# Attention weights times V in row tiles of 64, V with a bank of its own, and a new timetable for the attention stage

## What is computed

```python
x = x + xattn(layernorm(x), ctx, ctx, wq, wk, wv, wo)
x = x + ffn(layernorm(x), W_in, b_in, W_out, b_out)

# xattn: 16 heads of 16 channels
Q, K, V = queries @ wq, keys @ wk, values @ wv        # to (batch, head, channel, time)
corr = irfft(rfft(Q) * conj(rfft(K)))                 # over 128 positions
top_vals, top_idx = top_k(corr, 4)                    # for each head and channel
w = softmax(top_vals)
for i in range(4):                                    # a roll along the 16 channels
    out = out + w[..., i] * take_along(V, (t - top_idx[..., i]) % 16)
return out @ wo

# ffn: 256 -> 1024 -> 256, int8 weights and int16 activations by the largest magnitude of the whole tensor
hidden = gelu(quantize_a16(x) @ quantize_w8(W_in) + b_in)
out = quantize_a16(hidden) @ quantize_w8(W_out) + b_out
```

## Time and profile before

| | us |
|---|---|
| median of 3 runs | 1089.81 |
| lowest and highest | 1086.69, 1091.14 |
| the profiled execution, device time | 1087.63 |
| its span, first to last instruction | 1085.8 |
| share of the span: PE, DVE, ACT, POOL | 97%, 89%, 86%, 46% |
| stage A, to the last `project_out` | 0 to 596.3 |
| seam 1 | 596.3 to 604.95 |
| stage B | 604.95 to 829.0 |
| seam 2 | 829.0 to 835.0 |
| stage C | 835.0 to 1085.8 |

### The profile page before, as it was taken

How to read it: one execution, slowest core, us unless ns; L and a number is a source line. 1 busy time by engine, 2 the same in 40 slices (tenths; PEclk the granted TensorE clock), 3 DMA queues, 4 the chain that set the end, 5 groups by cost and what they waited for, 6 DMA issues and landing times.

```text
span 1085.8 us, 28919 instructions
## 1 busy us (share of the span) xinstructions
PE 1048.4 (97%) x9303; PEld 772.8 (71%) x9303; DVE 969.8 (89%) x2790; ACT 936.6 (86%) x1698; POOL 504.7 (46%) x674
## 2 busy tenths in 40 slices
PE   6999999999999999999998799999997999999998
PEld 4787878878888888888876344444444888888886
DVE  3799989898888888889899899999997999999998
ACT  4787989988888888888888688888888999999996
POOL 4787888888888888888887300000000000000000
PEclk9999999999999999999999899999998999999999
DMA  5533335443334333333431499999899899999995
GB/s 184 162 117 94 121 114 142 113 124 119 124 116 133 118 119 117 119 118 117 118 119 49 144 302 303 302 302 302 305 305 378 298 346 342 343 341 344 339 348 199
DMA packets 141425, 222.59 MB, mean 205 GB/s; under 512 B 72320, under 2 KB 92160, under 8 KB 137216
## 3 DMA queue, kind: packets, MB, share of 16 engines
q1 hardware_dynamic: 140224, 220.12, 60.7%
q10 hardware_dynamic: 1088, 1.05, 0.3%
HBM read 121.00 MB, written 83.89 MB: 189 GB/s over the span
## 4 chain that ended last, share of the span: by engine, by line
PE 59%; DVE 10%; issue 8%; ACT 2%; DVEq 1%; POOL 0%; ACTq 0%; POOLq 0%
PE bank L596 21%; DVE arena L1436 6%; PE bank L431 5%; PE bank L444 5%; PE bank L506 5%; PE bank L482 5%; PE bank L625 4%; PE bank L456 4%; PE bank L494 4%; PE bank L468 3%; PE bank L521 3%; DVE arena L1429 2%; DVE arena L1451 1%; ACT arena L891 1%; DVEq L1433 0%
## 5 line engine op out<-in xcount | busy, mean ns | idle before, releaser
L625 PE MATMUL bank<-wout,arena 128*128 128x256 f16 x2048 | 236.3, 274 | 4.2 <-DVE arena L1429 3.0
L625 PEld LDWEIGHTS bank<-wout,arena 128*128 128x128 f16 x2048 | 197.0, 98 | 45.0 <-DVE arena L1436 10.6
L596 PE MATMUL bank<-arena,win 128*128 128x512 f16 x1024 | 224.1, 383 | 2.6 <-DVE arena L1387 2.6
L596 PEld LDWEIGHTS bank<-arena,win 128*128 128x128 f16 x1024 | 100.6, 98 | 126.0 <-issue 6.2
L1436 DVE SCALAR_TENSOR_TENSOR arena<-arena,wout_rel 128x512 f16<-128x512 int16 x256 | 183.0, 746 | 3.9 <-ACT arena L891 1.3
L848 ACT ACTIVATE arena<-bank,b_in_sb,z_scale 128x512 f32<-128x512 f32 x192 | 147.4, 778 | 16.4 <-PE bank L596 11.2
L711 ACT ACTIVATE arena<-arena 32x128 f32<-32x128 f32 x256 | 78.4, 306 | 57.7 <-DVE arena L1166 55.4
L645 ACT ACTIVATE arena<-bank 128x512 f32<-128x512 f32 (+1 forms) x196 | 115.3, 590 | 6.3 <-PE bank L431 2.9
L884 ACT ACTIVATE arena<-arena,one 128x1536 int16<-128x1536 f32 x64 | 100.2, 1568 | 18.3 <-DVE arena L1436 15.3
L645 ACT ACTIVATE arena<-arena 128x512 f16<-128x512 f32 x192 | 112.9, 618 | 1.2 <-POOL arena L951 1.1
L1401 DVE TENSOR_REDUCE hmax<-arena 128x1 f32<-128x1024 f32 x96 | 111.2, 1211 | 2.9 <-ACT arena L848 2.9
(11 more groups left out here) (121 smaller groups left out, 2040.7 us busy)
## 6 DMA issues: line engine op xcount, KB each, us to landing
hidden_scratch<-arena SPq DMA_DIRECT2D x32, 1536.0 KB, 5.6
arena<-hidden_scratch SPq DMA_DIRECT2D x64, 768.0 KB, 7.1
arena<-in_ctx_turned SPq DMA_DIRECT2D x64, 256.0 KB, 2.7
arena<-in_x_turned SPq DMA_DIRECT2D x64, 256.0 KB, 2.8
arena<-in_x SPq DMA_DIRECT2D x64, 256.0 KB, 3.7
x_scratch<-arena SPq DMA_DIRECT2D x64, 256.0 KB, 3.5
arena<-x_scratch SPq DMA_DIRECT2D x32, 512.0 KB, 6.0
out<-arena SPq DMA_DIRECT2D x32, 512.0 KB, 4.3
```

Source lines behind the costliest of these rows:

```text
L596: last = nc.tensor.matmul(bank[f][:, :].rearrange("p (n t) -> p n t", n=4), win16[:, f, c, :], xt[q % 3][:, s, :, c, :], start=s == 0 and ...
L625: last = nc.tensor.matmul(bank[m * 2 + k // 2][:, k % 2 * D:(k % 2 + 1) * D], gbuf[:, s, f, k * P:(k + 1) * P], wout16[:, f, :], start=f = ...
```

## The change

`attend` becomes eight matmuls in place of four. The mixing matrix `mt` is zero outside blocks on its diagonal, so its upper and lower halves of 64 rows need only 64 columns each. Each half is a matmul with a contraction of 64, still with 128 columns of weights (V) but 64 moved columns. The upper half writes into the free columns 256 to 511 of bank 5, the lower into those of bank 6, and the two banks are now one PSUM tensor `both`, so that ScalarE can read the two halves in one instruction. V keeps bank 7 for itself.

```diff
-        bank = [ctx.enter_context(nc.psum_tensor(f"bank{n}", [P, 512], F32)) for n in range(8)]
+        both = ctx.enter_context(nc.psum_tensor("both", [P, 1024], F32))
+        bank = [ctx.enter_context(nc.psum_tensor(f"bank{n}", [P, 512], F32)) for n in (0, 1, 2, 3, 4, 7)]
+        bank[5:5] = [both[:, 0:512], both[:, 512:1024]]
+        mixed = lambda h: bank[5 + h][:, 2 * P:4 * P].rearrange("p (c b l) -> p c b l", c=2, b=2)
+        mixed_halves = both[:, :].rearrange("p (h s k l) -> p h s k l", h=2, s=2, k=4)[:, :, 1]
...
# project_v
-                wait(pe, S["ot_out"], upto(p - 3) if taken is None else taken)
...
# attend
-                wait(pe, S["vt_out"], upto(p + 4) if taken is None else taken)
+                wait(pe, S["top_done"], upto(p + 2) if taken is None else taken)
                 for c in range(DC):
                     for b in range(2):
-                        last = nc.tensor.matmul(four(7)[:, c, b, :], vt[:, p, c, b, :], mt[:, c, b, :], start=True, stop=True)
+                        for h in range(2):
+                            half_of = slice(h * NF, (h + 1) * NF)
+                            last = nc.tensor.matmul(mixed(h)[:, c, b, :], vt[half_of, p, c, b, :], mt[half_of, c, b, half_of], start=True, stop=True)
...
# inverse
+                wait(pe, S["ot_out"], upto(p - 1) if taken is None else taken)
...
# high_ot, and take_ot alike
-                copy(ot16[p % 2][:, 0].rearrange("p c b l -> p (c b l)"), bank[7][:, :], "ot_high")
+                copy(ot16[p % 2][:, 0].rearrange("p c b (h l) -> p h (c b) l", h=2), mixed_halves, "ot_high")
```

TensorE's step is put in another order with other lags:

```diff
-                if active(t, 0):
-                    project_k(t)
-                    project_v(t)
-                if active(t, 4):
-                    project_out(t - 4)
-                if active(t, 0):
-                    if t == 0:
-                        mean_of_wq()
-                    project_q(t)
-                if active(t, 3):
-                    attend(t - 3)
-                if active(t, 0):
-                    dft_k(t)
-                    dft_q(t)
-                if active(t, 1):
-                    inverse(t - 1)
+                if active(t, 5):
+                    attend(t - 5)
+                if active(t, 2):
+                    dft_q(t - 2)
+                    dft_k(t - 2)
+                if active(t, 3):
+                    inverse(t - 3)
+                if active(t, 1):
+                    project_k(t - 1)
+                    project_v(t - 1)
+                    project_q(t - 1)
+                if active(t, 5):
+                    project_out(t - 5)
```

The work on the feed-forward weights moves. On VectorE all of it falls into two steps, on ScalarE it is one operation a step over 24 steps:

```diff
-W_STEP = 6
+W_STEP = 4
...
# VectorE, weights(t)
+                if t == 2:
                     dve.wait_ge(S["w_in_loaded"], 16)
+                    for k in range(4):
+                        largest_w(w_in_raw, win_max, k)
+                    scales(win_max, win_up).then_inc(S["w_in_scaled"], 1)
+                if t == 3:
                     dve.wait_ge(S["w_out_in"], 16)
+                    for k in range(4):
+                        largest_w(w_out_raw, wout_max, k)
                     link(scales(wout_max, wout_up))
...
# ScalarE, weights(t)
+                k, r = (t - W_STEP) // 3, (t - W_STEP) % 3
+                if 0 <= k < 4:
+                    scaled_w_in(2 * k + r) if r < 2 else stage_w_in(k)
+                if 4 <= k < 8:
+                    scaled_w_out(2 * (k - 4) + r) if r < 2 else stage_w_out(k - 4)
```

TensorE gets matmuls whose result nobody reads: ten at the start, ahead of `mean_of_wq` (which now runs first, and `wq` is loaded second in place of third), 13 and 8 in seam 1, 4 and 10 in seam 2:

```diff
+            def keep_warm(n, k, table_of=None):
+                lhs, rhs = (minus_mean, minus_mean) if table_of is None else (inv16[:, 0, 0, :], inv16.rearrange("p s k t -> p (s k t)"))
+                for _ in range(k):
+                    nc.tensor.matmul(bank[n][:, 0:rhs.shape[-1]], lhs, rhs, start=True, stop=True)
...
+            pe.wait_ge(S["x1_done"], PAIRS)
+            keep_warm(0, 13, inv16)
             pe.wait_ge(S["xm_ready"], 1)
             spread_over_partitions(0, xm_part).then_inc(S["xmax_all"], 1)
-            pe.wait_ge(S["x1_done"], PAIRS)
+            keep_warm(0, 8, inv16)
...
             pe.wait_ge(S["b_gelu"], (QUADS + 1) * FC)
+            keep_warm(0, 4, inv16)
             pe.wait_ge(S["hmax_part"], 1)
             spread_over_partitions(0, hm_part).then_inc(S["hmax_all"], 1)
+            keep_warm(0, 10, inv16)
```

414 lines of the change are left out of this document (243 added, 171 removed).

## The result

The changed kernel takes 1094.44 us (median of 7 runs, 1093.22 to 1097.98) against 1086.69 for the kernel before (median of 7 runs beside it, 1086.28 to 1091.14): a ratio of 1.0064, 95% interval 1.0048 to 1.0080. It is slower by 0.6%; I had forecast 0.4% faster, most likely no change that can be measured. It is one of two of the seven runs (1097.71 and 1097.98, both at a mean granted clock of 0.993) that took longer than the other five (1093.22 to 1094.78, at 0.996 or 0.997).

The account below looks back on a forecast made before the run. Stage A was taken as bound by PE's instruction stream. The terms 3.1 - 5.2 + 1 + 0.8 - 2.8 - 0.8 gave -3.9 us, so 1086 us against the median of the runs, with a range from 1072 to 1102.

Parts of the forecast that it names:

- part 1: Attend in row tiles: bound by weight loads, plus one more tiling switch; +0.055 us a pair, +3.1 us over 57 steps.
- part 4: Ramp: earlier start, but DVE's chain carries weight work; sixth K projection at 52 against 50.70, +1 us, bounds -3 and +4.
- 8 pairs at 111 ns: Attend's 16 weight loads: the two row tiles load side by side, so eight pairs, each taking 111 ns.
- rival A: Attend: loads do not bind in row tiles, 0.39 us less a pair, -25 us more, 1061 us; chance 0.13.
- Part 2: Banks and waits in stage A: new waits on DVE and ACT have margins in hand, so they cost nothing.
- Rival D: Stage A: a hand-over between DVE and ACT fails, 0.3 us a step over 64 steps, +19, 1105 us; chance 0.14.
- Part 3: Feed-forward weight work in stage A: at most one such operation a step on ACT removes stretched steps, -5.2 us.
- Part 5: Last pairs of stage A: chain through DVE with less PE work to lay beside it, +0.8 us, bounds -2 and +4.
- Part 6: Seams: spare matmuls keep the clock at 2.4 GHz, -2.8 us at stage B's start and -0.8 in seam 2.

Follow-up runs that it names:

- The spread kernel with late loads: Changed kernel with VectorE's feed-forward weight work over steps 6 to 15, ScalarE's ten steps later, and 1 MB loads two steps later: 1088.32 us, ratio 1.0011.

## Why the prediction was wrong, by its own steps

Two steps failed by about as much each: part 1 by 5.2 us over its 57 steps (57 x 0.092), part 4 by 4.5 us at the sixth K projection.

**Part 1** failed in a term's size, the price of the switches of tiling. "8 pairs at 111 ns" and rival A's refutation were right: loads of 128 fp32 columns bind at 112 ns, side by side in the two tiles, with 64 or 128 moved columns. Attend took the 1.04 us that I gave it. But I had counted 0.11 us for the way in as part of these 1.04, and it lies in front of them: from the projection's last record to attend's first it is 0.20 us in place of 0.11, the first pair is followed by the second after 0.16 in place of 0.112, and the way out is 0.206, as it was before, where I took 0.149 (a last half stream and 0.094). That makes +0.147 us a pair instead of +0.055: +7.9 us in 54 steps against 3.0, and some 9.4 over all pairs. The experiment with the full array puts the whole of it down to the tiles. I had sized the switch at 0.1 us from the whole of a step's three switches; the price of each one would have had to be read off the gap in front of a piece and that between its first two records, separately.

**Part 2** was right: no wait appears on PE in the steady state, and the 1.2 us that DVE stands at `sum_ex` cost nothing. Rival D did not happen. **Part 3** was right as a sum (-5.1 against -5.2), and wrong in the share I later gave to ScalarE.

**Part 4** was +1 (the sixth K projection at 52), and it came at 56.49. The start was nearly as forecast (11.54 for 11). What failed behind it: first, the first inverse was to come at 22 and came at 25.46: I had moved the 1 MB load forward on SP without asking what it does to the small load behind it, and that load was on the path, through ACT's order. Second, the chain on DVE ended 3.0 us late (attend of pair 1 at 51.18, for 48.2), about what the inverse was late (3.5); the bunched work itself took 3.15 and 4.6 us where I had 4.7 and 4.1. Third, from there to the sixth K projection it took 5.31 us, not 3.75, at a clock partly at 1.2 GHz. I had taken the ramp's clock as 1.00 throughout, though a chain through DVE had to leave PE idle in it. 3.0 and 1.5 are the 4.5 us between forecast and result; my upper bound of +4 did not hold either (+5.8). The 3.75 itself was right at full clock: the kernel with twice the moved columns has it, at 1.00. So the 1.5 are the clock's, and of this execution: the four other kernels with bunched work show 1.00 behind that attend, and the sixth K projection at 53.3 to 54.8, still later than the forecast's 52. The spread kernel with late loads shows what the same timetable does otherwise: the sixth K projection at 47.45, 3.2 us earlier than before.

**Part 5**, +0.8 expected, +3.6 measured: 0.6 of it for the tiles (four pairs at 0.147), and the new chain costs 1.3 without them (51.13 against 49.86, with the full array, at full clock). The remaining 1.7 goes with the clock, which falls to 0.50 and 0.60 behind two waits of 1.4 us. No run was made for this, but the traces bear it out, by the mean clock of this stretch: with row tiles 52.22 us at 1.00 (twice the moved columns), 52.64 to 53.16 at 0.97 (three kernels) and 53.46 at 0.94; with the full array 51.13 at 1.00 and 52.41 at 0.97. The kernels with 64 x 64 tiles had 49.7, at 1.00.

**Part 6** was right for stage B (-2.6 for -2.8). Stage C gave nothing for -0.8: the clock is 1.00, PE needs less (9.14 us for 9.80), and ACT is busy for 9.80 of the 9.80 us, as I had read before and then not taken at its word. A quad bound by ACT does not get shorter with PE's clock.

With the terms as measured: 7.9 - 5.1 + 5.9 + 3.6 + 0.4 (seam 1, not explained) - 2.6 = +10.1 us, against a forecast of -3.9. The median of the runs is 3.3 below this execution, and that of the kernel before 0.9 below its own, so it is +7.8 between the medians. The forecast's 1086 stood on a median before of 1089.81 (3 runs); in the comparison it was 1086.69 (7 runs), so it is the difference of -3.9, not the 1086, that the result answers.

The Trainium skill, TensorEngine Tiling (Array Packing), section Theoretical Speedup, gives up to 2x where the contraction is at most 64. In this case no such gain is seen with fp32 tiles of 64 x 128 (1.04 us against 0.98), and 1.6x with 64 x 64 (0.63). The section LDWEIGHTS of its page TensorE: Matmul & The Clock Gate (columns, not rows, set a load) is what the runs bear out.

**The best kernels** found are those with 64 x 64 tiles, spread work and late loads, at 0.978 to 0.981 of the kernel before; they are faster than both kernels of this case. One with full-array tiles is at 0.992.

## What to carry to other kernels

Before splitting a matmul into smaller tiles, ask which side binds it: if the spacing of its records equals what its load costs by its columns (here 112 ns against the 110 that the loads' slope gives for 128 fp32 columns), cut the columns of the weights, not the rows or what is moved. When work is put into a ramp "because engines idle there", follow the one chain that the ramp consists of; a burst on the engine of that chain (here 7.7 us of work, 4.6 to 4.8 by the medians), or a large transfer issued ahead of a small one that it needs (here 1.0 to 1.2), is paid for, and in some executions once more by the clock, if it falls in the gap. And a budget by the starts of the same pieces in both traces, step by step, shows single stretched steps that a sum over fifty steps lays at the wrong door.

## What the hardware did that I had not expected

- Four 64 x 64 fp32 tiles start a round of four records every 58 ns (after the second), 7 ns from one to the next within a round; two 64 x 128 tiles a pair every 112 ns (after the second).
- Going from the full array to row tiles cost 0.09 us in front of the first record and 0.05 between the first pair and the second; going on from attend to the transforms took 0.20 to 0.21 us on the full array and in row tiles with 64 or 128 moved columns, but 0.148 with 64 x 64 tiles.
- With a load of 1 MB in flight, a load of 256 KB issued 3 us behind it landed after 5.7 to 6.9 us in five kernels, instead of 3.0 to 4.3 in the six that issue the large one later.
- A transposing load of one and the same tensor held SP for 2.4 to 2.9 us in some kernels and 4.2 to 4.9 in others; quarters of it took 1.2 to 1.3 each.
- The same wait did not always bring the same clock: behind an attend that had waited 1.62 us for VectorE, the granted clock from 52 to 56 us was 0.61 in one execution and 1.00 in another, of kernels that differ only in attend's moved columns.
